# The rows of maxima: issued by ScalarE behind its own copy, instead of by SP

## What is computed

```python
x = x + xattn0(layernorm(x), ctx)   # 32 heads of 16, 8 key/value heads, softmax over keys, Wo
x = x + ffn0(layernorm(x))          # x @ weight.T + bias, plus LoRA of rank 16 by batch
x = x + xattn1(layernorm(x), ctx)   # 16 heads of 32, softmax over the batch-and-head axis
x = x + ffn1(layernorm(x))          # x @ W_base.T + b_base + 0.5 * irfft of a low-rank update
```

## Time and profile before

| | us |
|---|---|
| median of 3 runs | 306.61 (304.91 to 307.49) |
| profiled execution, first to last instruction | 305.9 |
| TensorE busy | 294.3 (96%) |
| DVE, ScalarE, GpSimd busy | 232.8, 161.5, 147.8 |

### The profile page before, as it was taken

One profiled execution on the slowest core, in us unless ns is written; L12 is line 12 of the kernel. 1 busy time (PEld: TensorE's weight loads), 2 busy tenths in 40 slices (PEclk: granted clock), 3 DMA queues, 4 the chain that ended last, 5 costly groups with the idle time before them and its releaser, 6 DMA issues.

```text
span 305.9 us, 6265 instructions
## 1 busy us (share of the span) xinstructions
PE 294.3 (96%) x2150; PEld 231.3 (76%) x2150; DVE 232.8 (76%) x375; ACT 161.5 (53%) x277; POOL 147.8 (48%) x192
## 2 busy tenths in 40 slices
PE   5998899899999999999999999999999999999996
PEld 1876756657677467668898898898996767888885
DVE  3699498758895886764677687899788689988762
ACT  4964577396429645963335652565644274364220
POOL 6684620037121231471320078289356969886651
PEclk9999799999999999999999999999999999999999
DMA  7969929939941965004044024343156512000112
GB/s 246 308 197 193 175 75 156 205 87 130 154 116 40 155 94 117 3 2 157 2 133 110 1 70 137 97 120 105 36 138 191 162 57 74 2 0 36 70 71 103
DMA packets 32822, 33.08 MB, mean 108 GB/s; under 512 B 4294, under 2 KB 21958, under 8 KB 32792
## 3 DMA queue, kind: packets, MB, share of 16 engines
q1 hardware_dynamic: 32792, 32.69, 45.5%
HBM read 18.39 MB, written 2.10 MB: 67 GB/s over the span
## 4 chain that ended last, share of the span: by engine, by line
PE 80%; SPq 8%; DMA 6%; ACT 2%; POOL 1%; issue 1%; DVE 1%; ACTq 0%; POOLq 0%
PE ps L451 17%; PE ps L453 16%; PE ps L452 16%; PE ps L610 5%; PE ps L687 4%; PE ps L767 3%; PE ps L676 3%; PE ps L806 2%; SPq L574 2%; PE ps L655 2%; PE ps L695 2%; SPq L537 2%; PE ps L779 2%; DMA QS<-negmax 2%; DMA Q<-Q1d 1%; DMA QS<-Q_h 1%
## 5 line engine op out<-in xcount | busy, mean ns | idle before, releaser
L1356 POOL TENSOR_SCALAR var_eps<-moments 128x1 f32<-128x1 f32 x32 | 8.1, 252 | 76.0 <-DVE moments L1108 75.6
L1145 DVE TENSOR_REDUCE mx<-ps 128x8 f32<-128x1024 f32 x32 | 38.4, 1219 | 6.4 <-PE ps L655 6.1
L943 ACT ACTIVATE PT<-ps 128x1024 f32<-128x1024 f32 x32 | 32.1, 1022 | 15.5 <-PE ps L676 15.2
L451 PE MATMUL ps<-xT_h,slot_h 128*128 128x256 f32 x128 | 37.6, 293 | 0.5 <-POOL slot_l L1345 0.3
L452 PE MATMUL ps<-xT_l,slot_h 128*128 128x256 f32 x128 | 36.6, 286 | 0.0
L453 PE MATMUL ps<-xT_h,slot_l 128*128 128x256 f32 x128 | 36.5, 285 | 0.0
L1345 POOL TENSOR_TENSOR slot_l<-stg,slot_h 128x512 fp32r<-128x512 f32 x19 | 26.4, 1394 | 12.2 <-ACT slot_h L871 12.2
L896 ACT ACTIVATE xT_h<-ps 128x512 fp32r<-128x512 f32 x24 | 14.2, 596 | 25.2 <-PE ps L610 19.8
L1349 POOL TENSOR_TENSOR ctxT_l<-ctx_in,ctxT_h 128x512 fp32r<-128x512 f32 x11 | 14.4, 1309 | 24.9 <-ACT ctxT_h L880 24.8
L451 PEld LDWEIGHTS ps<-xT_h,slot_h 128*128 128x128 f32 x128 | 25.0, 195 | 1.7 <-issue 1.1
L1386 POOL TENSOR_TENSOR zpart<-P 128x512 f32<-128x512 f32 x16 | 22.0, 1376 | 7.1 <-ACT P L1010 5.9
(11 more groups left out here) (165 smaller groups left out, 865.3 us busy)
## 6 DMA issues: line engine op xcount, KB each, us to landing
ctx_in<-in_ctx SPq DMA_DIRECT2D x22, 256.0 KB, 3.4
QS<-Q_h SPq DMA_DIRECT2D x32, 128.0 KB, 4.9
Q<-Q1d SPq DMA_DIRECT2D x64, 64.0 KB, 2.1
X<-in_x SPq DMA_DIRECT2D x8, 256.0 KB, 3.9
stg<-in_wq SPq DMA_DIRECT2D x8, 256.0 KB, 3.3
QS<-Q_l SPq DMA_DIRECT2D x16, 128.0 KB, 4.9
out<-XB SPq DMA_DIRECT2D x7, 256.0 KB, 2.0
stg<-in_wo SPq DMA_DIRECT2D x4, 256.0 KB, 5.6
```

Source lines behind the costliest of these rows:

```text
L451: eng.matmul(dst, left[0], right[0], start=start, stop=False)
L943: act.activation(PT[:, g2, :], wide(step).rearrange("p k n -> p (k n)"), ACT.Exp, scale=SCALE0).then_inc(free(step), 1)
L1145: dve.tensor_reduce(mx[:, b % 2, :].rearrange("p (x r) -> p r x", r=REP)[:, r, :], wide(step).rearrange("p k (g t) -> p (k g) t", g=4), AX ...
```

## The change

DM.0 to DM.7 leave SP's list and stand in ScalarE's, each right behind MT.b. The code of the step moves along: ScalarE waits for its own copy (`consumed(act, ("MT", b))`) and issues the two transfers. With that the bookkeeping of PSUM is put by engine: in place of six counters `unit_free`, one per unit, there are two, `act_freed` and `dve_freed`, that count all releases by ScalarE and by DVE in the order of their lists. The units get the numbers of their banks (unit 5 is called 6; the place is the same). SP waits in addition for `la_copied` before it loads over the stage of la, and a few waits are written with counts taken from the lists (max_ready, fac_ready, fac_copied).

```diff
 SP_TEXT = """
...
-LC.0.2 LX.5 LC.0.3 LS LX.6 KL.0 LW.wo.1 QL.0 DM.0 LW.wo.2 LC.0.4 LW.wo.3 QL.1 LW.la.0 LC.0.5 DM.1 LW.lb.0 QL.2
-LW.w0.0 KL.1 LW.w0.1 DM.2 LW.w0.2 LC.0.6 QL.3 DM.3 LC.0.7 QL.4 KL.2 LC.1.0 QL.5 LW.w0.3 LW.wk1.0 DM.4 LW.wk1.1
-KL.3 DM.5 LW.wk1.2 QL.6 LW.wk1.3 DM.6 QL.7 LC.1.1 LW.wq1.0 DM.7 LW.wq1.1 LW.wq1.2 LE LC.1.2 LW.wq1.3 QX.0 QX.1
+LC.0.2 LX.5 LC.0.3 LS LX.6 KL.0 LW.wo.1 QL.0 LW.wo.2 LC.0.4 LW.wo.3 QL.1 LW.la.0 LC.0.5 LW.lb.0 QL.2
+LW.w0.0 KL.1 LW.w0.1 LW.w0.2 LC.0.6 QL.3 LC.0.7 QL.4 KL.2 LC.1.0 QL.5 LW.w0.3 LW.wk1.0 LW.wk1.1
+KL.3 LW.wk1.2 QL.6 LW.wk1.3 QL.7 LC.1.1 LW.wq1.0 LW.wq1.1 LW.wq1.2 LE LC.1.2 LW.wq1.3 QX.0 QX.1
...
 ACT_TEXT = """
...
-Q0.0.1 W.wo.0 CT.0.3 LNn.0.2 LNn.0.3 XT.0.3 XT.0.2 V0.3 V0.2 LNn.0.4 MT.0 W.wo.1 Q0.1.0 ST.0.3 W.wo.2 K0.1
+Q0.0.1 W.wo.0 CT.0.3 LNn.0.2 LNn.0.3 XT.0.3 XT.0.2 V0.3 V0.2 LNn.0.4 MT.0 DM.0 W.wo.1 Q0.1.0 ST.0.3 W.wo.2 K0.1
...
+ACT_FREES = {("S1",) + s[1:] if s[0] == "SM" else s: n for n, s in enumerate(
+    s for s in ACT_ORDER if s[0] in ("V0", "MT", "ST", "PV", "SM", "WM", "V1", "PV1"))}
...
         def consumed(eng, step):
-            eng.wait_ge(unit_free[UNIT[step]], USE[step] + 1)
+            if step in ACT_FREES:
+                eng.wait_ge(act_freed, ACT_FREES[step] + 1)
+            else:
+                eng.wait_ge(dve_freed, DVE_FREES[step] + 1)
...
         def take(eng, step):
-            if USE[step]:
-                eng.wait_ge(unit_free[UNIT[step]], USE[step])
+            by_act = [ACT_FREES[s] for s in BEFORE[step] if s in ACT_FREES]
+            by_dve = [DVE_FREES[s] for s in BEFORE[step] if s not in ACT_FREES]
+            if by_act:
+                eng.wait_ge(act_freed, max(by_act) + 1)
+            if by_dve:
+                eng.wait_ge(dve_freed, max(by_dve) + 1)
             return place(step)
...
+                        if old[0] == "la":
+                            sp.wait_ge(la_copied, 1)
...
-                elif kind == "DM":
-                    b = step[1]
-                    consumed(sp, ("MT", b))
-                    if b >= 2:
-                        all_filled(sp, stacks(b - 2))
-                    for e in range(2):
-                        row = e * HALF + STACK - 1
-                        sp.dma_start(QS[row:row + 1, b % 2, :, :].bitcast(F32),
-                                     negmax[...]).then_inc(max_loaded[b % 2], 16)
...
                     act.activation(negmax[0:KVH * REP, b % 2, :], place(step)[0:KVH * REP, 0:P], ACT.Copy,
-                                   scale=-1.0).then_inc(free(step), 1)
+                                   scale=-1.0).then_inc(act_freed, 1)
+                elif kind == "DM":
+                    b = step[1]
+                    consumed(act, ("MT", b))
+                    if b >= 2:
+                        all_filled(act, stacks(b - 2))
+                    for e in range(2):
+                        row = e * HALF + STACK - 1
+                        act.dma_start(QS[row:row + 1, b % 2, :, :].bitcast(F32),
+                                     negmax[...]).then_inc(max_loaded[b % 2], 16)
```

More of the change, by code:

```diff
@@ L143 @@
                  "S1", "V1", "PV1", "OX1", "F1", "FH", "WM", "WE")
[L144 to L147, removed]
+WIDE = ("MX", "ST", "S1")
+BANK = {step: bank for step, bank in PE_BANKS if step in FILLS}
+BEFORE, LAST_OF = {}, {}
+for step, bank in BANK.items():
+    mine = (bank, bank + 1) if step[0] in WIDE else (bank,)
+    BEFORE[step] = [LAST_OF[k] for k in mine if k in LAST_OF]
+    LAST_OF.update({k: step for k in mine})
+ACT_FREES = {("S1",) + s[1:] if s[0] == "SM" else s: n for n, s in enumerate(
+    s for s in ACT_ORDER if s[0] in ("V0", "MT", "ST", "PV", "SM", "WM", "V1", "PV1"))}
+DVE_FREES = {s: n for n, s in enumerate(
+    s for s in DVE_ORDER if s[0] in ("XT", "OX", "K0", "Q0", "MX", "OB", "WO", "F0", "OX1", "LT", "K1", "Q1", "V1", "F1", "FH", "WE"))}
 HALVES = numbered(ACT_ORDER, "CT", "K0", "XT", "Q0", "OX", "LT", "K1", "Q1")
@@ L158 @@
 NMS, NMS_POOL = numbered(DVE_ORDER, "NM"), numbered(POOL_ORDER, "NM")
+MAXIMA, FACTORS = numbered(DVE_ORDER, "S1"), numbered(DVE_ORDER, "FF")
+COPIED = {}
+for step in ACT_ORDER:
+    if step[0] == "FP":
+        for g in range(C * step[1], C * step[1] + C):
+            if ("NM", g) in NMS_POOL:
+                COPIED[g] = len(COPIED) + 1
 SUMS = numbered(POOL_ORDER, "XB")
@@ L304, in build @@
         psum_full = sem("psum_full")
-        unit_free = [sem(f"unit_free{k}") for k in range(NG + 2)]
+        act_freed, dve_freed = sem("act_freed"), sem("dve_freed")
         split_hi = sem("split_hi")
@@ L918, in _ @@
                                    place(step)[:, P:2 * P].rearrange("p (g d) -> p g d", g=KVH),
-                                   ACT.Copy).then_inc(free(step), 1)
+                                   ACT.Copy).then_inc(act_freed, 1)
                 elif kind == "Q0":
@@ L943, in _ @@
                     act.activation(PT[:, g2, :], wide(step).rearrange("p k n -> p (k n)"), ACT.Exp,
[L944 removed]
+                                   scale=SCALE0).then_inc(act_freed, 1)
                 elif kind == "PV":
@@ L949, in _ @@
                         filled(act, ("OB", b - 1, gq))
-                    act.activation(OTs[:, gq, :], place(step), ACT.Copy).then_inc(free(step), 1)
+                    act.activation(OTs[:, gq, :], place(step), ACT.Copy).then_inc(act_freed, 1)
                 elif kind == "OX":
@@ L1034, in _ @@
                     act.wait_ge(bv_ready, 1)
-                    act.activation(mt[:, :], place(step), ACT.Copy).then_inc(free(step), 1)
+                    act.activation(mt[:, :], place(step), ACT.Copy).then_inc(act_freed, 1)
                 elif kind == "BV":
@@ L1046, in _ @@
                     all_filled(act, [("K1", GROUPS - 1 - c) for c in range(C)])
-                    act.activation(V1[:, b, :], place(step), ACT.Copy).then_inc(free(step), 1)
+                    act.activation(V1[:, b, :], place(step), ACT.Copy).then_inc(act_freed, 1)
                 elif kind == "PV1":
@@ L1055, in _ @@
                         all_filled(act, [("S1", GROUPS - 2), ("S1", GROUPS - 1)])
-                    act.activation(O1T[:, n % 2, :], place(step), ACT.Copy).then_inc(free(step), 1)
+                    act.activation(O1T[:, n % 2, :], place(step), ACT.Copy).then_inc(act_freed, 1)
         @block.vector
@@ L1097, in _ @@
                     src = stage(key)
-                    dve.tensor_tensor(src, place(step), src, ALU.add).then_inc(free(step), 1)
+                    dve.tensor_tensor(src, place(step), src, ALU.add).then_inc(dve_freed, 1)
                 elif kind == "LNs":
@@ L1161, in _ @@
                     filled(dve, step)
-                    dve.tensor_tensor(X[:, b, :], place(step), X[:, b, :], ALU.add).then_inc(free(step), 1)
+                    dve.tensor_tensor(X[:, b, :], place(step), X[:, b, :], ALU.add).then_inc(dve_freed, 1)
                 elif kind == "LT":
@@ L1180, in _ @@
                             op0=ALU.mult, op1=ALU.add)
-                    last.then_inc(free(step), 1)
+                    last.then_inc(dve_freed, 1)
                 elif kind in ("K1", "Q1"):
@@ L1189, in _ @@
                         scalar=bias_qk[:, k, g % C:g % C + 1], in1=hi.bitcast(F32),
-                        op0=ALU.add, op1=ALU.subtract).then_inc(free(step), 1)
+                        op0=ALU.add, op1=ALU.subtract).then_inc(dve_freed, 1)
                 elif kind == "S1":
@@ L1204, in _ @@
                     low = M[:, (p + 1) % PAIRS, 0, :]
-                    dve.wait_ge(max_ready, C * (p + 1))
+                    dve.wait_ge(max_ready, max(MAXIMA[("S1", C * p + c)] for c in range(C)) + 1)
                     if p:
@@ L1278, in _ @@
                     dve.wait_ge(bv_loaded, 16)
-                    dve.tensor_tensor(V1[:, b, :], place(step), bv_all[:, :], ALU.add).then_inc(free(step), 1)
+                    dve.tensor_tensor(V1[:, b, :], place(step), bv_all[:, :], ALU.add).then_inc(dve_freed, 1)
                 elif kind == "BV":
@@ L1290, in _ @@
                     dve.wait_ge(xb_ready, n + 1)
-                    dve.tensor_tensor(XB[:, n % 2, :], place(step), XB[:, n % 2, :], ALU.add).then_inc(free(step), 1)
+                    dve.tensor_tensor(XB[:, n % 2, :], place(step), XB[:, n % 2, :], ALU.add).then_inc(dve_freed, 1)
                 elif kind == "FH":
@@ L1298, in _ @@
                     dve.tensor_tensor(XB[:, n % 2, cols], place(step)[:, 0:D // 2], XB[:, n % 2, cols],
-                                      ALU.add).then_inc(free(step), 1)
+                                      ALU.add).then_inc(dve_freed, 1)
                 elif kind == "WC":
@@ L1397, in _ @@
                     g = step[1]
-                    pool.wait_ge(fac_copied, sum(s[1] >= g // C * C for s in NMS_POOL))
+                    pool.wait_ge(fac_copied, COPIED[g])
                     pool.tensor_tensor(P1[:, g, :, :], P1[:, g, :, :],
```

84 lines of the change are left out of this document (40 added, 44 removed).

## The result

| | before | after |
|---|---|---|
| median of four runs each, us | 306.69 (304.91 to 307.49) | 315.06 (313.51 to 316.62) |
| profiled execution, first to last instruction | 305.9 | 314.8 |
| TensorE busy | 294.3 | 298.8 |

The ratio is 1.0303, with a 95% interval of 1.0255 to 1.0351: 8.4 us slower by the medians, 9.3 by the ratio. The forecast was 305.1 us with a range from 303.0 to 309.3, so the time lies outside it, on the slow side. Medians here are over all runs; a ratio leaves out the runs that are over 1.5% slower than the fastest of the same kernel.

The account below looks back on a forecast made before the run. TensorE was taken as the bound, full from 63 to 200 us and standing still 4.2 us from 20 to 63. Terms: -0.34 - 1.30 - 0.66 + 0.65 + 0.1 + 0.1 = -1.45, so 305.1 us; range 303.0 to 309.3.

Parts of the forecast that it names:

- Part 1, batch 0: First scores of batch 0: DM.0 lands earlier, leaving QL.0's landing as the limit; gain 0.34 us, at least 0.
- Part 1, batch 2: Scores of batch 2: from ScalarE the maxima land in 2 to 3 us, ending the wait; gain 1.30 us.
- Part 1, LC.0.6: Context of batch 6: LC.0.6 issued earlier, near 50 us, so WO.0's wait for V0.5 goes; gain 0.66 us.
- Part 2, d = 1.3: ScalarE's time lost per DM step: two issues 1.2 us plus 0.1 for its own write, eight times.
- DM.3, 0.65: Dense ScalarE stage behind DM.3: XT.0.6 comes late, a new TensorE wait of 0.65 us at L704 (OX.1).
- DM.5, 0.1: Behind DM.5: ST.4.1's exponential has slack 1.17 us, so the pause costs 0.1 us.
- Part 3, the counters at 0: PSUM counters per freeing engine: each wait met by the same instruction, cost 0, 0.2 us either way.
- the gain of the one half-clock stretch: Rival 1: the clock dip behind batch 0's wait goes too, 1.7 us gained, 303.4 us; chance 0.20.
- Rival 2: ScalarE's issues each wait for one of SP's, d is 2.5; +2.25 us, 308.9 us; chance 0.20.
- d = 2.5: High bound of ScalarE's pause per DM step, from SP's slowest pair; at DM.1 TensorE would be 0.9 us late.
- Rival 3: Maxima wait at the busy DMA engines as long as now, whoever issues; +0.2 us, 306.8 us; chance 0.18.
- the first paragraph: What bounds the kernel: TensorE waits only from 20 to 63 us, where the first attention's eight batches start; 4.2 us.

Follow-up runs that it names:

- e1: The changed kernel with all DM steps back in SP's list, only the new counters kept: 305.17 us, ratio 0.9986 to the kernel before.
- e2: The changed kernel, ScalarE issuing, with SP waiting at DM.b's old place for the copy of MT.b: 317.41 us, ratio 1.0380.
- e6: The changed kernel, ScalarE issuing, with SP held at DM.b's old place until both rows are issued: 309.22 us, ratio 1.0101.
- e4: The changed kernel with DM.0 and DM.2 back in SP's list, the other six on ScalarE: 309.70 us, ratio 1.0131.
- e7: The kernel before, SP issuing, with four extra unread copies on ScalarE behind each MT.b and no transfer moved: 310.14 us, ratio 1.0132.
- e3: The kernel before, with ScalarE also issuing the same transfers of maxima into rows nobody reads: 310.75 us, ratio 1.0156.
- e5: The changed kernel with only DM.0 and DM.2 on ScalarE, the other six back in SP's list: 312.59 us, ratio 1.0233.
- b8: The kernel before, SP issuing, with both rows of a batch in one transfer: 304.60 us, ratio 0.9966.
- e8: The changed kernel with both rows of a batch in one transfer, so one issue on ScalarE: 310.47 us, ratio 1.0127.

## Why the prediction was wrong

**Part 1, batch 0 (gain 0.34).** Wrong. The landing of QL.0 is a bound, and I took it that DM.0 would come down to it. It did not: QL.0 landed at about 31.25 and the later row at 32.95. That row was issued at 26.41 before and at 27.37 after, since MT.0 came 0.96 us later, and took 5.58 us and not 4.64; LW.wo.2 and LC.0.4 had gone out ahead of it and not behind it. The wait became 2.68 us. Whether the move did this stays open: e1, with SP issuing in the old order, has 5.37 us to land and a wait of 2.66 in its own profile.

**Part 1, batch 2 (gain 1.30).** The step that failed most. I priced DM.2 at "2 to 3 us to land" from the queue, and asked only what would now be *ahead of it in its own queue*. It took 6.97 us, longer than the 4.2 of the earlier trace rows, and the wait of 1.30 us, which was to go, became 3.11. I had seen that SP stood 28.2 us in front of L548 and read it as a delay of the loads behind. It was also what kept these loads behind the maxima. Freed, they went first (e2 and e6 against each other, 8 us). They did not go out earlier than before (LC.0.6 at 54.43, before 54.55). It was ScalarE that was later: MT.2's copy ended at 55.8 and not at 52.5, because of the later start, the longer wait at batch 0 and the half clock behind it. In the kernel before, SP's wait would have moved the loads back with the maxima; now nothing did.

**Part 1, LC.0.6 (gain 0.66).** The wait for V0.5 went, as predicted. But LC.0.6 was issued at 54.43, against 54.55 before, and not near 50: QL.2 needs DVE's half of Q0.1.1, for which SP waited 4.8 us, and went out at 44.24 (before 43.47). With TensorE 6.8 us later at MT.3, LC.0.6 was in time. e1, e4 and e7, in which SP issues DM.2, do not have this wait either, nor that of 1.30 us at batch 2: both gains were counted on waits that the one profile of before shows and not every run has.

**Part 2, d = 1.3.** Right: pairs took 1.15 to 1.25 us, and 1.3 passed between ScalarE's copy and its next operation. DM.1 and DM.2 cost no wait, as said. **DM.3, 0.65**: 0.71 measured, by the steps of the working, with 0.21 more ahead of it at ST.2.1. **DM.5, 0.1**: here the term is mis-sized, since I looked at the wrong reader. I checked the exponential ST.4.1. The tight one is PV.4.1, directly behind MT.5: its copy frees PSUM unit 3, which WO.3 takes. ScalarE and TensorE in the kernel before:

```profile
96.08 0.57 ACT L950 ACTIVATE OTs<-ps 128x512 f32<-128x512 f32 x1
```

```profile
96.87 0.48 PE L451 MATMUL ps<-slot_h,OT_h 128*128 128x512 f32 x1
```

The copy was done at 96.65, and WO.3 began at 96.87: a slack of 0.2 to 0.3 us and not 1.17. 1.3 less that is the wait of 0.99 that the changed kernel shows and e2, e3, e4 and e7 repeat. ST.7.3 (0.1) came 0.4 late and MX.7.0, which I had at 0, 0.5 to 0.7 late in e4 and e6. From MT.3 to OX.7 TensorE takes 75.4 to 75.7 us in e1, e5 and b8, where SP issues here; it takes 78.5 in the changed kernel, 78.4 in e7 and 79.1 in e4. So the pause costs 2.7 to 3.4 us by the profiles and about 4 by the ratios of e4 and e7. I had 0.85.

**Part 3, the counters at 0.** Right (e1: 0.9986).

**The clock.** I weighed only the gain of the one half-clock stretch. That longer waits bring more of them stood in no rival: in the profile three stretches of 3.41 us in place of one, 3.4 us, and by the mean clocks none or one more in the other three runs. By e5's clocks this is about half of what the late maxima cost, an estimate.

**The rivals.** Rival 2 had the sign, through issues that wait for each other. No pair of the changed kernel took over 1.25 us, though, so this is not what it lost. Slower pairs exist, mostly at DM.1: 2.40 us before and 2.09 in e5 on SP alone, 2.31 on SP and 2.17 on ScalarE in e3, where both issued at 42.28, and 2.22 in e6; at DM.6 1.63 in e6, while SP issued nothing. Where ScalarE's pair at DM.1 was that slow, TensorE waited for DVE's maxima as Part 2 has it for d = 2.5: 0.9 there, 0.73 in e3 and 0.78 in e6. What makes the pairs slow stays open. Rival 3 was right that the maxima come no earlier, and wrong that they would come no later. The missing rival was: *the transfers that stood behind the maxima overtake them*. Its price could have been had from the earlier trace rows: LC.0.6, issued right behind DM.2 and LW.w0.2, took 6.9 us where DM.2 took 4.2, and a row issued behind them would have fared like it. One reading of the first paragraph is wrong as well: only the maxima of batches 0 to 3 fall between 20 and 63 us (MT.7 begins at 117.87), so half of the DM steps stood in the stretch where TensorE never waited.

## What to carry to other kernels

A queue that stands in front of a small, urgent transfer also holds back the big ones behind it. Before you move such a transfer, write down what is issued next on the old queue once it is free, and price the small one as if it stood behind that. On the engine that takes the issues over, look at each step behind them for the PSUM unit or tile that it frees and at who takes it next; at DM.5 the tightest step was the first one behind, and I had checked a later one. If a transfer has to be issued by a compute engine, make it one and not two (e8), and hold the others back until it is out, not until it may go (e6 against e2).

## What the runs showed of the hardware that I had not expected

- The same 8 KB from SP's and from ScalarE's queue, issued at the same moment while the 16 DMA engines were busy (share 1.03 and 0.91 in those two stretches of e3), landed within 0.4 us of each other (4.6 and 4.8 us at batch 0; 4.2 and 3.8 at batch 2). In the changed kernel, behind about 1 MB issued in the 2.5 us before, they took 6.97 us; at DM.3, with a DMA share of 0.02, 1.8.
- Two DMA issues kept ScalarE from its next operation for 1.3 us. Most pairs took 1.15 to 1.25 us, a few 1.5 to 2.2. One transfer for both rows took 0.51 to 0.53 us in e8, but for its first, 1.12.
- Small waits of TensorE can have a second price: behind the waits of 2.68 and 3.11 us its granted clock was 0.50 for 6.83 and for 3.41 us. The length of the wait alone does not tell: behind 1.72 us before and 2.66 in e1 it was 0.50 for 3.41 us, and behind 1.95 us in e4 and 1.30 before it stayed at 1.00.
